# Layer 1 of a two-layer cross-attention and mixture-of-experts kernel: expert weights as the stationary operand in most blocks, token columns two blocks ahead, second products three steps behind

## The reference

```python
router_logits = x_flat @ router_w.T
top_k_logits, top_k_idx = jax.lax.top_k(router_logits, TOP_K)
router_probs = jax.nn.softmax(top_k_logits, axis=-1)
hidden = jnp.einsum('nc,ecd->ned', x_flat, w1_all)
hidden = jnp.square(jax.nn.relu(hidden))
out_all = jnp.einsum('ned,edc->nec', hidden, w2_all)
sel = jnp.take_along_axis(out_all, top_k_idx[:, :, None], axis=1)
out = jnp.sum(sel * router_probs[:, :, None], axis=1)
```

## Time and profile before

| | us |
|---|---|
| median of 3 runs (691.18 to 691.99) | 691.21 |
| the profiled execution, its own time | 698.34 |
| its span, first to last instruction | 696.5 |
| layer 1's blocks in it, first up to last down | 578.85 to 673.5 |
| PE busy in the span | 641.9 (92%) |
| DVE, ACT, POOL busy | 386.9, 336.9, 268.3 |

### The profile page before, as it was taken

One profiled execution on the slowest core, in us unless ns is written; L12 is line 12 of the kernel. 1 busy time (PEld: TensorE's weight loads), 2 busy tenths in 40 slices (PEclk: granted clock), 3 DMA queues, 4 the chain that ended last, 5 costly groups with the idle time before them and its releaser, 6 DMA issues.

```text
span 696.5 us, 18912 instructions
## 1 busy us (share of the span) xinstructions
PE 641.9 (92%) x6536; PEld 506.7 (73%) x6536; DVE 386.9 (56%) x1262; ACT 336.9 (48%) x675; POOL 268.3 (39%) x501
## 2 busy tenths in 40 slices
PE   8899999899999999999999999879999999989960
PEld 5667777667999999999995555557777766768630
DVE  3778899864443322232223222568999896744317
ACT  4566566442455455545531112458777643434420
POOL 5662555533232121112111111214477555866540
PEclk9999999999999999999999999999999999999995
DMA  9144555651123111111115000611122135454219
GB/s 230 38 151 140 165 193 171 207 185 47 62 85 92 39 32 39 36 35 33 39 54 132 32 17 16 209 50 33 62 72 70 63 109 138 148 161 124 81 58 357
DMA packets 50478, 69.74 MB, mean 100 GB/s; under 512 B 7751, under 2 KB 37831, under 8 KB 50387
## 3 DMA queue, kind: packets, MB, share of 16 engines
q1 hardware_dynamic: 41276, 49.66, 23.1%
q0 software_dynamic: 6528, 17.90, 7.2%
q10 hardware_dynamic: 2583, 0.98, 0.6%
HBM read 46.28 MB, written 22.23 MB: 98 GB/s over the span
## 4 chain that ended last, share of the span: by engine, by line
PE 71%; DVE 14%; issue 5%; DMA 5%; POOL 2%; ACT 1%; SPq 1%; another core or an unknown queue 1%; DVEq 0%; POOLq 0%; ACTq 0%
PE ps L1993 17%; PE ps L2049 17%; PE ps L1977 12%; DVE m_rows L1179 4%; PE ps L1763 4%; PE ps L1718 3%; PE ps L1701 3%; PE ps L1755 3%; PE ps L1801 2%; DVE x_sb L1163 2%; PE ps L1777 2%; PE ps L1729 1%; DVE ctx_q L1196 1%; DMA xs_dram<-xn,slot_now 1%; PE ps L2025 1%
## 5 line engine op out<-in xcount | busy, mean ns | idle before, releaser
L2049 PE MATMUL ps<-w_all,share 128*128 (+3 forms) x576 | 137.6, 382 | 3.3 <-ACT w_all L1062 2.1
L718 POOL DMA_INDIRECT ys_dram<-share,dest_i x36 | 37.6, 1044 | 204.1 <-DVE share L1538 203.8
L2049 PEld LDWEIGHTS ps<-w_all,share 128*128 128x128 f32 (+3 forms) x576 | 97.5, 179 | 22.6 <-issue 6.7
L1977 PE MATMUL ps<-w_all,share 128*128 (+1 forms) x336 | 97.5, 430 | 3.8 <-DVE share L1325 3.3
L686 POOL DMA_INDIRECT xs_dram<-xn,slot_now x64 | 66.3, 1036 | 68.0 <-PE ps L1764 15.5
L1993 PEld LDWEIGHTS ps<-share,w_att 128*128 128x128 f32 x768 | 89.4, 192 | 1.3
L1993 PE MATMUL ps<-share,w_att 128*128 128x128 f32 x768 | 89.6, 275 | 0.0
L1977 PEld LDWEIGHTS ps<-w_all,share 128*128 128x128 f32 (+1 forms) x336 | 53.2, 166 | 36.9 <-issue 10.4
L1179 DVE TENSOR_REDUCE m_rows<-ps 128x8 f32<-128x960 f32 x64 | 70.5, 1142 | 12.0 <-PE ps L1718 11.8
L1322 DVE SCALAR_TENSOR_TENSOR xid<-share,be 128x1 f32<-128x1 f32 x36 | 7.8, 217 | 74.8 <-PE ps L1801 60.1
L1011 ACT ACTIVATE share<-ps 128x512 f32<-128x512 f32 x24 | 14.3, 598 | 69.4 <-PE ps L1993 69.4
(11 more groups left out here) (266 smaller groups left out, 1326.0 us busy)
## 6 DMA issues: line engine op xcount, KB each, us to landing
w_all<-ys_dram SPq DMA_DIRECT2D x16, 512.0 KB, 7.1
w_all<-gate SPq DMA_DIRECT2D x8, 688.0 KB
w_all<-up SPq DMA_DIRECT2D x8, 688.0 KB
w_all<-down SPq DMA_DIRECT2D x8, 640.0 KB
w_all<-w SPq DMA_DIRECT2D x16, 256.0 KB
share<-xs_dram SPq DMA_DIRECT2D x28, 129.0 KB
w_all<-xs_dram SPq DMA_DIRECT2D x28, 129.0 KB
out<-x_sb SPq DMA_DIRECT2D x8, 256.0 KB, 5.5
```

What stands on the lines that cost most here:

```text
L718: g.indirect_dma_start(ys_dram, bass.IndirectOffsetOnAxis(ap=dest_i[:, w:w + 1], axis=0), block_y(l, j), None).then_inc(stored(l, j)[0], 16)
L1977: i = t.matmul(ps[0:r, bank, 0:w], xgT[:, k, 0:r], w_all[:, bass.ds(off + (k * UPW[l] + col - EW[l]), w)], start=(k == 0), stop=(k == KT - 1))
L2049: i = t.matmul(ps[0:n, 6, 0:D], h[:, 0:n], w_all[0:r, bass.ds(off + (KT * UPW[l] + c * D - EW[l]), D)], start=(c == 0), stop=(c == KD[l] - 1))
```

## The change

Six things, by engine and place:

1. In layer 1, blocks 2 to 12 and 18 to 27 (21 blocks) are done with the weights as the stationary operand: `up_held` multiplies four 128x128 pieces of weights with 128 token columns moving. The result is the hidden columns, so DVE squares straight into `hT`, and `h_t1` and `hT_evac` are left out for these blocks. The stationary pieces are read from a buffer of six blocks, `held_w`, which SP fills with one DMA of 256 KB a block behind the block's row load; the expert's address comes from a second register read.
2. Two buffers for the token columns; `block_t` and `x_evac` run two blocks ahead (one at blocks 0 and around 13 to 17), and the copy comes ahead of the token numbers, in both layers.
3. h_t1(j-2) and down(j-3) in step j in place of h_t1(j-1) and down(j-2), three places in `hT`.
4. From block 5 of layer 1 on two result banks, 6 and 2 in turn.
5. The last block of layer 0 has columns (`hT_last`) and a result bank (3) of its own, and its transposes stand between the halves of down(34).
6. At layer 1's start: values two to a bank, PE's wait for e_y behind the keys, the fifth sequence's values behind the first q_proj; and the first result load of both combines split in two, one a tile.

```diff
@@ -135,7 +135,9 @@
+        hT_last = share[:, 2144:2912].rearrange("p (c n) -> p c n", c=6)
...
+        xgT_odd = share[:, 2656:2912].rearrange("p (k n) -> p k n", k=KT)
@@ -250,6 +252,7 @@
+        D_first = [D_gl[0], sem("results_loaded0_tile1")]
@@ -322,7 +325,7 @@
-        BANK_V = (6, 7, 5)
+        BANK_V = ((6, 0), (6, 1), (7, 0), (7, 1), (5, 0), (4, 0), (7, 0), (7, 1))
@@ -355,8 +358,11 @@
-            n = [sum(1 if i < FULL else 2 for i in range(j % NSEM, z, NSEM)) for z in (BLOCKS, j + 1)]
-            return n[0] * l + n[1]
+            def of(layer, i):
+                return (1 if i < FULL else 2) + (1 if layer == 1 and by_weights(1, i) else 0)
+            whole = sum(of(0, i) for i in range(j % NSEM, BLOCKS, NSEM))
+            return whole * l + sum(of(l, i) for i in range(j % NSEM, j + 1, NSEM))
@@ -381,22 +387,57 @@
-        WS0 = (4, BLOCKS)
+        WS0 = (4, 2)
...
-            return WS0[l] <= j < FULL
+            return WS0[l] <= j < FULL and not (l == 1 and N1 <= j <= REJOIN)
...
+        assert (BLOCKS - 1) % U3 == U3 - 1 and 2144 + 6 * P <= 2400 + (U3 - 1) * DX
+        def h_cols(l, j):
+            return hT_last if l == 0 and j == BLOCKS - 1 else hT
+        TWO_Y = 5
+        def y_bank(l, j):
+            if l == 1:
+                return 2 if j >= TWO_Y and j % 2 else 6
+            return 3 if j == BLOCKS - 1 else 6
+        def x_cols(l, j):
+            return xgT_odd if l == 1 and j % 2 else xgT
+        REJOIN = N1 + 4
+        def next_blocks(j):
+            def ahead(i):
+                return i + 1 if i < 1 or N1 - 2 <= i < REJOIN else i + 2
+            done = ahead(j - 1) if j else 0
+            return [b for b in range(done + 1, ahead(j) + 1) if b < BLOCKS]
...
+        held_at = (NE - 3) * EW[0] + RING * DX
+        held_w = w_all[:, held_at:held_at + NSEM * KT * HID[1]].rearrange("p (u k n) -> p u k n", u=NSEM, k=KT)
+        assert held_at + NSEM * KT * HID[1] <= kv_at
+        def hT_at(j):
+            return KD[1] * (j % 3)
@@ -491,6 +532,14 @@
+                    if l == 1 and by_weights(1, j):
+                        if j >= WS0[1] + NSEM:
+                            sp.wait_ge(b_up, 4 * BLOCKS + j - NSEM + 1)
+                        first_row = sp.value_load(woff_i[0:1, j:j + 1], min_val=EW[1], max_val=NE * EW[1])
+                        sp.dma_start(held_w[:, j % NSEM, :, :],
+                                     experts[1][0].rearrange("e i (q n) -> (e i q) n", q=HID[1] // 64)[
+                                         bass.ds(first_row - EW[1], EW[1]), :].rearrange(
+                                             "(k p q) n -> p k (q n)", k=KT, p=P)).then_inc(L_xg[j % NSEM], 16)
@@ -545,7 +594,11 @@
-                for b in range(NB):
+                for t in range(QT):
+                    sp.dma_start(yg[:, 0, t, :, :].rearrange("p k d -> p (k d)"),
+                                 ys_dram[t * P * TOPK:(t + 1) * P * TOPK, :].rearrange(
+                                     "(p k) d -> p (k d)", k=TOPK)).then_inc(D_first[t], 16)
+                for b in range(1, NB):
@@ -1030,8 +1083,9 @@
-                    need(a, b_y, j)
-                    a.copy(hT[:, 0:4, :], ps[:, 4, 0:4 * P].rearrange("p (c n) -> p c n", c=4)).then_inc(e_hT, 1)
+                    if j < BLOCKS - 1:
+                        need(a, b_y, j)
+                    a.copy(h_cols(0, j)[:, 0:4, :], ps[:, 4, 0:4 * P].rearrange("p (c n) -> p c n", c=4)).then_inc(e_hT, 1)
@@ -1051,24 +1105,24 @@
-                    need(a, b_y, BLOCKS + j - 1)
-                    a.copy(hT[:, KD[1] * (j % 2):KD[1] * (j % 2) + KD[1], :],
+                    need(a, b_y, BLOCKS + j - 2)
+                    a.copy(hT[:, hT_at(j):hT_at(j) + KD[1], :],
...
-                    a.copy(block_y(1, j), ps[:, 6, 0:D]).then_inc(e_y, 1)
+                    a.copy(block_y(1, j), ps[:, y_bank(1, j), 0:D]).then_inc(e_y, 1)
...
-                    if j >= 1:
-                        hT_evac(j - 1)
-                    if j >= 2:
-                        y_evac(j - 2)
+                    if j >= 2 and not by_weights(1, j - 2):
+                        hT_evac(j - 2)
+                    if j >= 3:
+                        y_evac(j - 3)
@@ -1080,6 +1134,8 @@
+                        hT_evac(j - 1)
+                        y_evac(j - 2)
@@ -1154,21 +1210,24 @@
-                    v.wait_ge(D_gl[b], 16 * (L + 1))
+                    if b:
+                        v.wait_ge(D_gl[b], 16 * (L + 1))
...
+                            if b == 0 and k == 0:
+                                v.wait_ge(D_first[t], 16 * (L + 1))
...
-                def values(B, bank):
+                def values(B, bank, at_=0):
...
-                    v.tensor_tensor(value_rows(b)[:, :, 0:3:2, :], ps[0:K, bank, 0:D].rearrange("p (g s d) -> p g s d", s=2, d=DH),
+                    v.tensor_tensor(value_rows(b)[:, :, 0:3:2, :], ps[0:K, bank, at_ * D:(at_ + 1) * D].rearrange("p (g s d) -> p g s d", s=2, d=DH),
@@ -1318,11 +1377,11 @@
+                    need(v, b_up, 4 * j if l == 0 else 4 * BLOCKS + j - 1)
+                    v.tensor_copy(x_cols(l, j)[:, :, :], ps[:, 2 if j == 0 else 7, 0:KT * P].rearrange("p (k n) -> p k n", k=KT)).then_inc(e_x, 1)
...
-                    need(v, b_up, 4 * j if l == 0 else 4 * BLOCKS + j)
-                    v.tensor_copy(xgT[:, :, :], ps[:, 2 if j == 0 else 7, 0:KT * P].rearrange("p (k n) -> p k n", k=KT)).then_inc(e_x, 1)
@@ -1340,12 +1399,12 @@
-                        values(B0 + b, BANK_V[b % 3])
+                        values(B0 + b, *BANK_V[b])
...
-                        values(B0 + b, BANK_V[b % 3])
+                        values(B0 + b, *BANK_V[b])
@@ -1354,8 +1413,8 @@
-                    values(B0 + 6, 4)
-                    values(B0 + 7, 5)
+                    for b in range(6, NB):
+                        values(B0 + b, *BANK_V[b])
@@ -1535,7 +1594,7 @@
-                    v.tensor_copy(block_y(0, j), ps[:, 6, 0:D]).then_inc(e_y, 1)
+                    v.tensor_copy(block_y(0, j), ps[:, y_bank(0, j), 0:D]).then_inc(e_y, 1)
@@ -1628,28 +1687,39 @@
-                    if not first:
+                    if not first and not last:
...
-                    need(v, b_y, j)
-                    v.tensor_copy(hT[:, 4, :], ps[:, 5, 0:P])
-                    if first:
-                        v.memset(hT[0:HALF, 5, :], 0.0)
-                    v.tensor_copy(hT[HALF:LAST_K, 5, :], ps[0:REST, 5, P:2 * P]).then_inc(e_hTv, 1)
+                    if not last:
+                        need(v, b_y, j)
+                    v.tensor_copy(h_cols(0, j)[:, 4, :], ps[:, 5, 0:P])
+                    if first or last:
+                        v.memset(h_cols(0, j)[0:HALF, 5, :], 0.0)
+                    v.tensor_copy(h_cols(0, j)[HALF:LAST_K, 5, :], ps[0:REST, 5, P:2 * P]).then_inc(e_hTv, 1)
...
+                        y_evac(j - 1)
...
                 def blk1(j, u, first, last):
-                    if not last:
-                        if j + 1 == N1:
-                            v.wait_ge(d_l2, LIST2 + 17)
-                        if j + 1 == FULL:
-                            v.wait_ge(d_l2, 2 * LIST2)
-                        x_evac(j + 1)
+                    def some_x(blocks):
+                        for n in blocks:
+                            if n == N1:
+                                v.wait_ge(d_l2, LIST2 + 17)
+                            if n == FULL:
+                                v.wait_ge(d_l2, 2 * LIST2)
+                            x_evac(n)
+                    some_x(next_blocks(j)[:1])
...
-                    v.wait_ge(b_hT, 2 * OLD0 + j - 1)
-                    v.tensor_tensor(h_pair[:, j % 2, :], act_pair[:, j % 2, :], act_pair[:, j % 2, :], ALU.mult).then_inc(e_h, 1)
+                    if by_weights(1, j):
+                        v.wait_ge(b_y, BLOCKS + j - 2)
+                        squares = hT[:, hT_at(j):hT_at(j) + KD[1], :].rearrange("p c n -> p (c n)")
+                    else:
+                        need(v, b_hT, 2 * OLD0 + by_tokens(1, j - 1) if j else 0)
+                        squares = h_pair[:, j % 2, :]
+                    v.tensor_tensor(squares, act_pair[:, j % 2, :], act_pair[:, j % 2, :], ALU.mult).then_inc(e_h, 1)
+                    some_x(next_blocks(j)[1:])
@@ -1681,12 +1751,14 @@
-                def v_proj(B, bank):
-                    b = B % NB
-                    t.wait_ge(a_ctx, 4 * l + 2 * (b // 4) + 2)
-                    for k in range(KT):
-                        i = t.matmul(ps[0:K, bank, 0:D], ctxT[:, k, b, :], w_att[:, 2, k, :], start=(k == 0), stop=(k == KT - 1))
-                    i.then_inc(p_v, 1)
+                def v_proj(B, bank, n=1):
+                    t.wait_ge(a_ctx, 4 * l + 2 * ((B + n - 1) % NB // 4) + 2)
+                    for at_ in range(n):
+                        b = (B + at_) % NB
+                        for k in range(KT):
```

(83 more changed lines are left out.)

## The result

The changed kernel took 701.61 us (median of four runs, 700.52 to 702.65), the kernel before, in the same job, 691.6: a ratio of 1.0145, 95% interval 1.0132 to 1.0157, or 10 us. The forecast was 693.5, range 686.5 to 698.0: the direction was right, the size was not. The profiled execution took 700.52, span 698.8.

A forecast was written before the change was run, and what follows sets the result against it. PE was taken as the bound in the steady stretches, block 13's late rows excepted. Terms, with the boundary's minus 2.05 inside SP's plus 3.2, summed to plus 2.6 on 691.2; with 0.3 for DVE's order, 693.5 us, range 686.5 to 698.0.

The forecast's parts named there:

- (a) to (c): Layer boundary: down(35) unblocked, minus 0.85; first result load halved, minus 0.35; one sequence's values behind first q_proj, minus 0.85.
- SP ahead of block 13: SP's queue before block 13: 11 added weight DMAs delay padding writes and block 13's load; plus 3.2, containing the 2.05.
- rival of cheap issues: SP's queue before block 13: weight DMAs cost little, 0.52 each, scatters stay last; minus 5.4, 685.8 us; chance 0.27.
- SP behind block 13: Blocks 18 to 27: SP needs 2.42 each against PE's 1.95, eating its lead until block 28; plus 1.0.
- minus 2.6 for PE: PE behind block 13: 13 h_t1 due instead of 25, saving 12 x 0.22; minus 2.6.
- steps 18 to 27 wait for weights: Layer 1, behind block 13: a sign that, if seen in the profile after, would show the forecast wrong.
- SP as slow as in its second stretch: Rival for blocks 13 to 28: 26 issues at 1.41 cost 6.8 more; 700, or 697 at half; chance 0.15.
- Clock, plus 1.75: At block 13: PE waits some 8 us for rows, then a step at 1.2 GHz takes 3.93 instead of 2.17.
- The first load in halves: First result load of both combines: one of four combine operations starts ahead; minus 0.35 at the boundary and again at the end.
- List step, one more product and the end: Behind block 13: list work step minus 0.4, one more down plus 0.86, waits at the end minus 1.1.
- DVE's order: Copy ahead of the token numbers on DVE: costed at nothing, gain at most 0.1 to 0.3; 0.3 in the final sum.
- The pause: 614.15 to 619: unexplained 4.40 us in the profiled execution of the kernel before; 5.4 too much, left out on both sides.

The follow-up runs named there:

- d2: Changed kernel with no block held and the first result load in halves only at the layer boundary; 693.13 us, ratio 0.9956 to the kernel before.
- e2: Changed kernel with no block held, first result load in halves only at the layer boundary, run in another job; 696.24 us, ratio 0.9965 to the kernel before.
- b4: Changed kernel with no block held and the first result load whole again; 692.23 us, ratio 1.0008 to the kernel before.
- b1: The changed kernel itself, run again beside variants on one chip; 701.56 us, ratio 1.0151 to the kernel before.
- b2: Changed kernel with the weights on a semaphore of their own, waited for by the held product alone; 700.45 us, ratio 1.014 to the kernel before.
- e1: Changed kernel with only blocks 18 to 27 held, weights issued by ACT, first result load halved only at the boundary; 694.23 us, ratio 0.9942 to the kernel before.
- b3: Changed kernel with all 21 weight DMAs issued by SP but unused and unwaited, products by tokens; 700.25 us, ratio 1.0145 to the kernel before.
- c1: Changed kernel with SP's weight DMAs unused and unwaited, each 32 KB instead of 256 KB; 700.15 us, ratio 1.0016 to the kernel before.
- a1: Changed kernel with no block of layer 1 held; 697.73 us, ratio 0.999 to the kernel before.
- d4: Changed kernel with all 21 blocks held, weights issued by ACT, first result load halved only at the boundary; 695.18 us, ratio 0.9982 to the kernel before.
- a3: Changed kernel with only blocks 18 to 27 held; 699.06 us, ratio 0.9993 to the kernel before.
- c2: Changed kernel with all 21 blocks held, weights issued by ACT instead of SP; 698.3 us, ratio 1.0 to the kernel before.
- c3: The kernel before itself, unchanged, run again for a profile; 699.56 us.
- d3: Changed kernel with small unused weight DMAs on SP, without their register read; 695.22 us, ratio 0.9982 to the kernel before.
- d1: The changed kernel itself, run again in another job; 703.09 us, ratio 1.010 to the kernel before.

## Why the prediction was wrong, point by point

**Boundary (a) to (c), minus 2.05.** About right where it was forecast: the queries' product started at 450.13 (454.03 before), 3.9 earlier, and the row loads at 573.17, 2.25 before the 575.42 of the earlier trace rows. How much of it reaches block 13 a single profile can't tell: d2 and e2, one kernel, started their row loads at 571.95 and 574.57, and loaded block 13 at 604.34 and 607.13; b4 started its row loads at 575.50, no earlier than the kernel before.

**SP ahead of block 13, plus 3.2.** Right. 24 issues took 28.8 us (forecast 28.9). Block 13's load went at 611.37, 1.1 after the forecast, since the five padding writes started 0.3 earlier but took 0.9 more (5.96 against 5.10), and the last landed after 3.02 and not 2.5; b1 against b4 gives 3.0. The rival of cheap issues is refuted: the weight DMAs cost SP some 1.26 each, above its 1.05. The forecast asked of blocks 11 and 12 only whether their weights come in time; block 3's did not, and PE waited 2.67. b2, without this wait, took 1.1 us less, within the intervals: the slack ahead of block 13 took most of it. The 2.6 us that the prediction estimates for 256 KB come from figures which the Trainium skill (DMA: Bandwidth & Descriptors, Anatomy of one DMA) gives for DMAs issued by GpSimd; SP issues these, and 4.12 was measured beside the row loads.

**The failed step: SP behind block 13, "plus 1.0", and with it the minus 2.6 for PE.** The forecast took PE as the bound behind block 13, so that its saving counts in full, and SP as a small addition. b1 took 51.3 us where b4 took 48.4. With 13 transposes less (2.8) and 0.2 more of product that is 5.5 us of lateness. The clock is 1.5 of it: blocks 13 to 18 took 12.20 in b1 (612.52 to 624.72) and 11.34 in b4, where three more transposes (0.65) stand between them. Some 4.0 remain, all behind block 18, where 1.0 was said. e1, whose weights ACT loads, gives the same: from block 18 to block 35 it took 35.2 us (624.04 to 659.27), b1 39.1. The prediction had named the sign itself, that steps 18 to 27 wait for weights: PE waited 0.30 at block 25 and 1.13 at block 27, and 1.16 for rows at block 32.

The term's inputs were low by a little each. In b1 the rows of blocks 13 to 17 went every 1.22 (forecast 1.15), the ten pairs every 2.50 (2.42), and the second half of block 28 went at 642.61 where 641.4 was forecast. A half load was priced at 1.15 like a whole one; it takes 0.48 to issue and not 0.33, and the next comes 1.3 later. Landing was taken as 2.5 for a half load and 3.0 for weights; it was 3.00 and 4.12 where PE waited (medians in b1 2.1 and 3.7). Together they made a bound of what should have been "asks at nearly their time". b3 shows that it was one: level with b1 with all transposes in place. How much of the 4.0 is SP's time and how much the longer landing stays open (c1). The rival "SP as slow as in its second stretch", at 0.15, came nearest in time, 700, but by luck: it rests on 1.41 an issue, and the 26 issues from block 13 to 28 were 1.25 apart in b1 (610.15 to 641.31).

**Clock, plus 1.75.** Right in kind (0.53 in 614 to 617) and nearly in size: 1.5 in b1. But PE's wait ahead of it was forecast at some 8 us and was 3.83; in b2, without the wait at block 3, it was 4.63.

**The first load in halves.** Minus 0.35 at the boundary was low (1.0, above); at the end the sign was wrong. The forecast counted what the second half does for tile 1, not that one more issue and transfer stands ahead of sequence 1: DVE waited 2.29, and the end was 0.8 us longer in b1 than in b4 (from the first result load's issue, 677.86 and 671.93, to the spans' ends, 698.2 and 691.5).

**The rest.** List step, one more product and the end, minus 0.64 together and 0.3 for DVE's order: b4 shows no gain, 1.0008 (0.9996 to 1.002). The last scatter started 1.8 us behind PE's end in b4 and 1.2 in the kernel before: POOL's scatters took back 0.6 of the 1.1 that was forecast for the end.

**The pause.** Taken out on both sides; that fits the profiles of the changed kernel and of b1 to b4, which have none. The account of profiles gives 3.0 + 2.9 + 0.8 = 6.7 of the 9.3 between the medians of b1 and b4; both profiled executions lie towards each other, 1.6 below and 1.1 above their medians. The other 2.6 us are in no profile, and what makes them was not seen.

## What to carry to other kernels

A DMA from a queue that also carries row loads costs its register read and address work too, and these can be more than the issue; price it by the distance between starts, for each shape apart, and follow the queue to its last consumer, not to the first. When work is taken from one engine and an issue given to another, ask for every stretch which of the two is the bound afterwards; holding ten blocks gained 2.0 us with the issues on an engine that had room, in the stretch where PE was the bound; holding 21 with the issues on SP lost 9.3 (b1 against b4).

## What the hardware showed

- A row load of 64 partitions (64.5 KB) takes SP 0.48 us to issue, one of 128 partitions (129 KB) 0.33, a weight DMA of 256 KB 0.38 and of 32 KB 0.33.
- In the four jobs in which the kernel before takes 696 to 699, ACT in many profiles runs one instruction every 2.2 to 2.9 us for a while behind block 13 (614.81 and 617.09 above, and alike in a1 and d4), with nothing in the trace that it waits for, and PE then waits 2.6 to 3.8 us (a1, a3, c2, c3, d4, e2). c1, d3 and the changed kernel (d1) show no such wait in these jobs, and neither do the profiles after and b1 to b4, from the jobs at 691. It may account for part of the 5 to 7 us by which the kernel before differs; that and its cause were not shown.
- The clock fell towards 1.2 GHz (0.57 over 583 to 587) behind a wait of 2.67 us, and was back at 2.4 GHz from 587.
- The Trainium skill (DMA: Bandwidth & Descriptors, Issuing engines are not separate DMA queues) says that the time to initiate a DMA is usually small beside the transfer. The trace differs: some 1.2 us of SP a weight DMA, the same for 32 KB and 256 KB, a third of its landing (4.12), and the queue pays it again for each. By that rule the rival of cheap issues, a gain, would have come true.
